# A decoder of two post-norm layers on one core: regrouped feed-forward weights, base products moved ahead, and transfers put behind the transposed input

## The reference

```python
x = _layernorm(x + _L0_attn_ref(...))   # down to 128, gelu, two passes of a bidirectional state-space mixer
                                        # with a 7-tap causal convolution, up to 512
x = _layernorm(x + _L0_xattn_ref(...))  # cross attention over the context joined with x: 16 heads of 96, 4 key heads
x = _layernorm(x + _L0_ffn_ref(...))    # gate, up (512 to 1792), silu, down; weights (int - zero) * scale
x = _layernorm(x + _L1_attn_ref(...))   # self attention, 32 heads of 16, alibi
x = _layernorm(x + _L1_xattn_ref(...))  # cross attention over the context: 32 heads of 128, 8 key heads, rms norms
x = _layernorm(x + _L1_ffn_ref(...))    # x @ W.T + b, plus a rank-16 adapter mixed over 8 experts by a router
```

## Time and profile before

| | us |
|---|---|
| median of 3 runs | 1679.01 |
| lowest and highest | 1676.1 and 1681.4 |
| the profiled execution, its own time | 1680.96 |
| its span, first to last instruction | 1679.2 |

### The profile page before, as it was taken

The page is one execution under the profiler, slowest core; times in us unless marked ns, Lnnn a source line. Parts: engine busy times, 40 slices in busy tenths (PEclk is TensorE's granted clock), DMA queues, the critical chain, the costliest instruction groups (busy, mean ns, idle before and its releaser), DMA issues. The chain is left out here.

```text
span 1679.2 us, 29888 instructions
## 1 busy us (share of the span) xinstructions
PE 1575.3 (94%) x11188; PEld 1316.2 (78%) x11188; DVE 932.6 (56%) x1647; ACT 803.6 (48%) x2447; POOL 769.3 (46%) x625
## 2 busy tenths in 40 slices
PE   6999999999997699998999879999999999999978
PEld 3777897888886488878777678888888888888866
DVE  3847503333365778775667734555555555555755
ACT  3342325444443355536999724454454454544520
POOL 3403214343421788842533545555555545554423
PEclk9999999999999799999999999999999999999999
DMA  6100200010102552203000031101101101100001
GB/s 207 38 1 1 57 20 20 20 41 2 52 2 82 182 175 98 79 1 120 1 2 26 29 113 38 39 26 38 46 19 51 38 27 39 32 26 14 1 1 51
DMA packets 62258, 77.85 MB, mean 46 GB/s; under 512 B 12136, under 2 KB 41316, under 8 KB 62116
## 3 DMA queue, kind: packets, MB, share of 16 engines
q1 hardware_dynamic: 61652, 74.63, 13.9%
q0 software_dynamic: 464, 1.32, 0.3%
HBM read 73.85 MB, written 2.10 MB: 45 GB/s over the span
## 5 line engine op out<-in xcount | busy, mean ns | idle before, releaser
L1145 POOL TENSOR_TENSOR xa_rs<-xa_ms,minus_half 128x5 f32<-128x5 f32 x64 | 74.7, 1168 | 170.0 <-DVE xa_ms L1395 169.9
L1151 POOL TENSOR_TENSOR xa_prob<-xa_prob,xa_inv 128x512 f32<-128x512 f32 x64 | 66.7, 1042 | 136.2 <-DVE xa_inv L1362 136.2
L763 POOL TENSOR_TENSOR xa_prob<-xa_prob,xa_inv 128x1024 f32<-128x1024 f32 x32 | 60.7, 1896 | 140.8 <-DVE xa_inv L1023 140.8
L1342 ACT ACTIVATE xa_prob<-xa_prob,xa_peak 128x128 f32<-128x128 f32 x256 | 99.7, 391 | 41.9 <-DVE xa_peak L1406 41.9
L1390 DVE TENSOR_REDUCE xa_ssq<-pre 128x4 f32<-128x512 f32 x64 | 43.9, 686 | 135.6 <-ACT pre L1328 135.6
L1699 DVE SCALAR_TENSOR_TENSOR ff_acc<-ff_ring,ff_sT,ff_acc 128x512 f32<-128x512 f32 x140 | 100.4, 747 | 21.6 <-ACT ff_acc L1653 12.7
L1599 PE MATMUL ff_ring<-xT_hi,ff_w 128*128 128x512 f32 x224 | 91.7, 410 | 18.1 <-DVE ff_acc L1699 13.5
L100 PE MATMUL xa_qp<-late_q_hi,xT_hi 128*128 128x512 f32 x256 | 107.2, 419 | 0.0
L1328 ACT ACTIVATE pre<-xa_qp 128x512 f32<-128x512 f32 x64 | 38.2, 597 | 142.6 <-PE xa_qp L102 142.6
L100 PE MATMUL xa_rows<-late_o_hi,xa_out_hi 128*128 128x512 f32 x256 | 102.6, 401 | 1.9 <-DVE xtok L1369 1.9
L2092 ACT ACTIVATE pre<-pre,sa_peak 128x128 f32<-128x128 f32 x256 | 99.2, 397 | 9.5 <-DVE sa_peak L2131 9.3
(11 more groups left out here) (415 smaller groups left out, 5054.6 us busy)
## 6 DMA issues: line engine op xcount, KB each, us to landing
pre<-in_wq SPq DMA_DIRECT2D x8, 1024.0 KB, 5.8
late_raw_o<-in_wo SPq DMA_DIRECT2D x8, 1024.0 KB, 5.2
ff_dn_q<-in_down_w SPq DMA_DIRECT2D x7, 512.0 KB, 3.8
ff_dn_z<-in_down_z SPq DMA_DIRECT2D x7, 512.0 KB, 4.9
ff_dn_s<-in_down_s SPq DMA_DIRECT2D x7, 512.0 KB, 6.1
pre<-in_wq SPq DMA_DIRECT2D x16, 192.0 KB, 3.5
pre<-in_wo SPq DMA_DIRECT2D x16, 192.0 KB, 3.9
pre<-in_xT SPq DMA_DIRECT2D x2, 1024.0 KB, 13.7
```

What stands on the lines that cost most here:

```text
L763: pool.tensor_tensor(prob[:, t % 3, :, :], prob[:, t % 3, :, :], bc(inv[:, t % 3, :], 2, [P, Q, KEYS]), ALU.mult).then_inc(s["norm"], 1)
L1145: pool.tensor_tensor(rs[:, :], ms[:, :], m.minus_half[:, 0:Q + 1], ALU.pow).then_inc(s["rs"], 1)
L1151: pool.tensor_tensor(prob[:, u % 2, :, :], prob[:, u % 2, :, :], bc(inv[:, u % 2, :], 2, [P, Q, S]), ALU.mult).then_inc(s["norm"], 1)
L1342: last = act.activation(prob[:, u % 2, h, :], prob[:, u % 2, h, :], ACT.Exp, bias=peak[:, u % 2, h:h + 1], accum_out=total[:, u % 2, h:h + 1])
```

## The change

It touches all six stages.

- Mixer: SP waits for the second half of `xT` (x1) before it issues `xtok`, `w_up` and `b_up`; POOL issues `taps` last, behind its small transfers and the constants, and after the same wait.
- First cross attention: the value weights are split in four pieces, the first products wait piece by piece, four fillers in place of nine.
- Feed-forward: the turns are grouped (0), (1, 2), (3, 4), (5), (6) in place of (0, 1), (2, 3), (4, 5), (6), so that there are 40 `out_rows` (16 of 12 matmuls, 24 of 6) in place of 32; SP issues the gate and up weights of turn T+1 ahead of the down weights of T; the weights' pieces are tied to units by two written tables; the first groups wait for turn 0's pieces one by one, two fillers in place of seven.
- Self attention: the output weights are split by DVE at the stage's head, no longer by ScalarE and POOL behind the first values.
- Second cross attention: the first key and value weights are split in two pieces; POOL's early pieces are spread over its steps 0 to 7; two fillers in place of five, and none in place of the 20; the base products of batches 0 to 3 of the last feed-forward replace the fillers at the end, one of them standing where there was no filler, in four banks that the two stages share.
- Last feed-forward: low rank first, then base(4), four `adapted`, and the rest in turn, five banks; the scaling of the norm is done by ScalarE, with a small shift from DVE (one column).

```diff
@@ hydra_stage, SP and POOL
                 sp_.dma_start(w_xbc[:, :], io["in_wT"][:, DIN:DIN + CONV]).then_inc(ld["in"], 16)
+                sp_.wait_ge(ld["x1"], 16)
                 sp_.dma_start(m.xtok[:, :, :], io["x"].rearrange("b s d -> s b d")).then_inc(ld["up"], 16)
...
-                pool.dma_start(taps[:, :, :], io["conv_w"].partition_broadcast(P)).then_inc(ld["conv"], 16)
                 pool.dma_start(conv_b[:, :], io["conv_b"].partition_broadcast(P)).then_inc(ld["small"], 16)
...
                 pool.memset(m.ones[:, :], 1.0).then_inc(s["consts"], 1)
 
+                pool.wait_ge(ld["x1"], 16)
+                pool.dma_start(taps[:, :, :], io["conv_w"].partition_broadcast(P)).then_inc(ld["conv"], 16)
                 pool.wait_ge(ld["conv"], 16)
@@ cross0_stage, TensorE (ScalarE and DVE split by c in the same way)
-                idle_products(pe, m, turn[:, 0:P], 9)
-                pe.wait_ge(s["v_lo"], 1)
+                idle_products(pe, m, turn[:, 0:P], 4)
                 for b in range(B):
-                    values_of(item(b)[:, 0:FEATS], m.cT_hi, m.cT_lo, b).then_inc(s["pre_mm"], 1)
+                    values_of(item(b)[:, 0:FEATS], m.cT_hi, m.cT_lo, b, b == 0).then_inc(s["pre_mm"], 1)
@@ ffn0_stage
-TABLE = [(hb, k) for hb in range(2 * math.ceil(TILES / GROUP)) for k in range(min(GROUP, TILES - GROUP * (hb // 2)))]
+GROUPS = ((0,), (1, 2), (3, 4), (5,), (6,))
+HALVES = 2 * len(GROUPS)
+TABLE = [(hb, k) for hb in range(HALVES) for k in range(MT * len(GROUPS[hb // 2]))]
...
-        mid = {n: [n - LAG] for n in range(LAG, 25)}
-        end = {}
-        mid[25], end[25], mid[26], end[26], mid[27], end[27] = [20, 21], [22], [23], [24], [25], [26, 27]
+        mid = {3: [0, 1], 4: [2, 3], 5: [4, 5], 6: [6, 7], **{n: [n - 1] for n in range(9, 22)}, 22: [22], 23: [24, 25], 24: [26, 27],
+               25: [28, 29], 26: [30, 31], 27: [32, 33]}
+        end = {21: [21], 22: [23], 27: [34, 35]}
...
+        weight_units = {1: (1, 1, 2, 2), 2: (3, 4, 4, 5), 3: (6, 7, 8, 9), 4: (10, 11, 12, 13), 5: (14, 15, 16, 17), 6: (18, 19, 20, 21)}
+        down_units = {0: (1, 1, 1, 2, 2, 2), 1: (3, 3, 4, 5, 5, 6), 2: (7, 7, 7, 8, 8, 8), 3: (10, 10, 11, 12, 12, 13),
+                      4: (14, 14, 15, 16, 16, 16), 5: (18, 18, 19, 20, 20, 21), 6: (22, 22, 23, 24, 24, 25)}
...
                 for T in range(TURNS):
+                    if T < TURNS - 1:
+                        if T >= 2:
+                            sp.wait_ge(s["w"], KC * (T - 1))
+                        elif T == 1:
+                            sp.wait_ge(s["w_first"], KC)
+                        ffn_stage_inputs(sp, io, *stage[(T + 1) % 2], T + 1, s["ld_even" if T % 2 else "ld_odd"])
                     if T:
-                        if T >= 3:
-                            sp.wait_ge(s["w"], KC * (T - 2))
-                        elif T == 2:
-                            sp.wait_ge(s["w_first"], KC)
-                        ffn_stage_inputs(sp, io, *stage[T % 2], T, s["ld_odd" if T % 2 else "ld_even"])
                         sp.wait_ge(s["dn_sub"], T)
                         sp.wait_ge(s["dn_w"], MT * T)
@@ cross1_stage, POOL's steps
-                        split_o(0, 2 * t)
-                        split_o(0, 2 * t + 1)
-                    if g <= G:
+                        split_o(0, t)
+                    if t == 2:
+                        split_o(0, 2)
+                        split_o(0, 3)
+                    if t == 3:
+                        split_kv(1, 0)
+                        split_kv(1, 1)
+                    if 4 <= t < B:
+                        split_q(1, b - 4)
+                        split_o(1, b - 4)
+                    if 1 < g <= G:
@@ cross1_stage, TensorE: unit 2, and behind the last unit
-                        idle_products(pe, m, rows[:, 0:P], 20)
+                        idle_products(pe, m, rows[:, 0:P], 0)
...
                 scores(UNITS - 1)
+                base(0, "qn", UNITS)
                 out_rows(UNITS - 3)
...
-                idle_products(pe, m, qp[:, 0:P], 9)
+                pe.wait_ge(s["kn"], UNITS)
+                base(1, "v_lo", UNITS)
                 out_rows(UNITS - 2)
...
-                idle_products(pe, m, qp[:, 0:P], 6)
+                base(2, "qT", UNITS)
                 out_rows(UNITS - 1)
                 turn_batch(UNITS - 2)
-                idle_products(pe, m, qp[:, 0:P], 14)
+                base(3, "masked", UNITS)
                 turn_batch(UNITS - 1)
@@ self_stage, DVE (taken from ScalarE and POOL)
+                dve.wait_ge(s["ld_o"], 16)
+                dve.tensor_copy(wo_hi[:, :, :], raw_o).then_inc(s["o_hi"], 1)
+                dve.wait_ge(s["o_hi"], 1)
+                dve.tensor_tensor(wo_lo[:, :, :], raw_o, raw(wo_hi[:, :, :]), ALU.subtract).then_inc(s["o_lo"], 1)
@@ lora_stage, TensorE and ScalarE
-                for b in range(1, B):
+                base(EARLY)
+                for b in range(EARLY):
+                    adapted(b)
+                for b in range(EARLY + 1, B):
+                    adapted(b - 1)
                     base(b)
-                    adapted(b - 1)
                 adapted(B - 1)
...
+                for b in range(B):
+                    act.wait_ge(s["shift"], b + 1)
+                    act.activation(m.xtok[:, b, :], m.xtok[:, b, :], ACT.Identity, bias=shift[:, b:b + 1],
+                                   scale=m.rstd[:, b:b + 1]).then_inc(n5["x"], 1)
```

More of the change, by code:

```diff
@@ L1061, in cross1_stage @@
         out_hi, out_lo = (sb(n, [P, 2, Q, S], F32R) for n in ("out_hi", "out_lo"))
-        qp, kvp, qt, kt, score, turn, mixed, rows = (pb(n) for n in ("qp", "kvp", "qt", "kt", "score", "turn", "mixed", "rows"))
+        qp, kvp, qt, score = m.late.bank
+        kt, turn, mixed, rows = (pb(n) for n in ("kt", "turn", "mixed", "rows"))
         s = {n: sem("xa1_" + n) for n in (
@@ L1643, in _ @@
                     turn(b)
-                    out_rows(28 + b)
+                    out_rows(LATE + b)
                 for b in range(4, B):
@@ L2179, in lora_stage @@
         low = [pb(f"low{i}") for i in range(2)]
-        rows = [pb(f"rows{i}") for i in range(BANKS)]
-        small, turned = pb("small"), pb("turned")
+        rows = [*m.late.bank, pb("rows4")]
+        small = pb("small")
+        turned = small[:, P:P + B]
+        shift = sb("shift", [P, B])
         s = {n: sem("lo_" + n) for n in (
-            "chain", "q", "logits", "lg", "exp", "wide", "wide_T", "route", "low", "t", "t_hi", "t_lo", "res", "rows", "add", "stored")}
+            "chain", "q", "logits", "lg", "exp", "wide", "wide_T", "route", "low", "t", "t_hi", "t_lo", "res", "rows", "add", "shift", "stored")}
         n5 = norm_sems(sem, "n5")
```

146 lines of the change are left out of this document (83 added, 63 removed).

## The result

The changed kernel takes 1653.26 us (median of 4 runs, 1649.81 to 1653.92), the kernel before 1677.78. The forecast was 1646.0, its range 1637 to 1656. The profiled execution of the changed kernel took 1649.81 us, its span is 1648.0.

A forecast was written before the change was run, and what follows sets the result against it. TensorE, busy 94% of the span, was taken as the bound, with gains only where it waits, runs fillers or runs slowly. Terms -2.7 - 2.3 - 9.8 + 0 - 9.2 - 9.0 = -33.0 gave median 1646.0 us, range 1637 to 1656.

The forecast's parts named there:

- Mixer's head: Mixer start: without taps in front the transposed input lands 2.9 us earlier, the residual about on the edge; -2.7 us.
- First cross attention: Its head: with value weights in quarters TensorE starts at about 172.1 in place of 174.33; -2.3 us.
- the signs: What the changed profile would show, such as first product at 11.5 to 12 and first values 2.3 us into their stage.
- Feed-forward: Its head, the largest term: earlier weights shorten the waits, fillers at 730.8 in place of 740.6; -9.8 us.
- the next hold: Feed-forward units 7 to 9: POOL's five instructions each in 7 and 8 delay row 8; 6.3 us lost.
- Self attention: Two instructions, some 3.6 us, move to DVE, which waits there; POOL loses one nothing waited for; 0 us.
- Second cross attention's head: Earlier start 1.0, unit 2's wait for POOL 6.9, clock behind it 1.5, less 0.2; -9.2 us.
- Joint and end: Last two stages: base products replace fillers; second cross attention ends 3.3 us later, the kernel's end 9.0 us earlier.
- signs that were to show it wrong: A residual landing after 28, a wait in units 10 to 27, or bases running at 0.43 us a matmul.
- more comes back: Rival: POOL's hold in feed-forward units 7 to 9 is hidden, -6 us, giving 1639 to 1641; chance 0.12.
- the hold only moves: Rival: feed-forward down weights land at 550, turns up to 3 wait, gain 3 for 9.8: 1653; chance 0.12.
- clock: Rival: with fewer fillers TensorE stands idle and its clock falls, 7 us at four places: 1653; chance 0.10.

The follow-up runs named there:

- taps_first: The changed kernel with the taps issued as POOL's first transfer again, SP's wait kept: 1653.64 us (one run).
- again: The changed kernel measured once more without an edit: 1651.84 us (5 runs), ratio 0.9838 to the kernel before.
- res_early: The changed kernel with SP's wait taken out, so the residual input is not held back; taps stay behind their wait: 1650.68 us, ratio 0.9833.
- mixer_hold: Changed kernel with residual step at second pass's head, POOL's context low parts behind first-pass roots, down-weight steps of turns 1 and 2 spread: 1645.92 us.

## Why the prediction came out as it did

The forecast of -33.0 stands against -27.0 over many profiles and -26.7 in the medians. By its own steps:

- **Mixer's head, -2.7: measured -1.0, and that is luck.** The start was right: 10.5 to 11.9 us in place of 14.56 and 13.67, in the mean 11.2 for 14.1, the 2.9 of the text, and `taps_first` shows that the taps are the cause. The context's transfer moved with it (issued at 20.99 for 23.80). What failed is "the residual is then complete at 24.5 to 25": it came at 27.5 to 28.65 where DVE waited for it, near the bound of 28.8 that the text gave. And the step did not ask what POOL's 4.44 us do to DVE when they move from 18 to 24 us. The text gave `w_conv` "until the convolution" and looked at TensorE alone. `again` and `res_early` show the hold, 4.20 and 3.67 us. So the second pass begins at 94.8 in the mean, before and after: the head gave nothing. The 1.0 lies behind it, where the first profile of before takes 75.9 us, with a clock of 0.50 from 125 to 130, and the other eight 73.8 to 74.1.
- **First cross attention, -2.3: measured -2.0**, by the mechanism named: 360.88 to 360.93 in eleven profiles, 362.43 in one, whose head ran at the lower clock (363.06 and 363.09 before). The first values stand 1.15 us into the stage, as 172.1 in the sum has it; the 2.3 among the signs is the gain and not this time.
- **Feed-forward, -9.8: measured -7.3, 6.8 when undone.** The start, DVE's wait at the down weights (forecast 2.6, measured 1.3) and TensorE's behind it (4.6; 3.20 to 4.83 in eight profiles) came where the text had them, DVE's half as long, and so did the next hold: row 3 ends 34.7 us into the stage, 34.0 by the text. The hold is a little larger: from row 7's end (576.65) to row 8's (597.99) are 21.3 us for 60 matmuls (14.0), 7.3 lost where the term had 6.3, and 0.5 more between rows 3 and 7. That profile's stage is 8.2 shorter than before. The mean is 1.2 longer than it, by the clock behind row 8's wait, low in five of eight profiles; the term had none.
- **Self attention, 0: measured +0.2.** The +1.4 of the two profiles is the clock, since both kernels show both lengths, the long one with 0.83 where the short one has 1.00.
- **Second cross attention's head, -9.2: measured -8.1** (656.76 - 651.97 + 3.3). The two key/value halves brought the first product forward by 0.97. The release by POOL gave 7.0, 6.9 expected (11.6 to 4.6 us from the root). The 1.5 us for the clock were right in size (627.02 against 625.45 behind the release in the two profiles of before) but read from one execution: of three profiles with the fillers and the old steps two have the low clock (0.57 and 0.58) and one has 1.00, so that part is worth about 1.0 on average. The rest that is missing lies ahead of POOL's root: the first transposed probabilities stand 22.3 to 22.5 us into the stage in four profiles and 23.6 to 23.8 in seven, and in `again` some of the first products (seven from 4.5 us into the stage on) take 0.43 us each where they take 0.23 in the first profile.
- **Joint and end, -9.0: measured -8.7.** The second cross attention's end was +3.3 in the profiles, as forecast. From first product to last sum are 25.1 to 25.2 us, the forecast's 25.1, in five of ten profiles, and 26.25 in the other five. The difference is how long the first products of low rank run at 0.43 us each: 4.8 us in the first profile, 3.1 in `again`.

The 6.0 us too much are thus the mixer (1.7), the feed-forward (2.5), the head of the second cross attention (1.1) and small parts. Of the signs that were to show it wrong, three came in part: the residual landed after 28 in four of the six profiles in which DVE waits for it, TensorE waits 0.66 us for POOL's low part in unit 17 (648.24), and the low-rank products, though not the bases, ran at 0.43 us. The rest of the distance from 1646.0 to 1653.26 is that the median of four runs lies 1.2 us above that of all nine. Of the rivals, *more comes back* is refuted; *the hold only moves* and *clock* each describe a part of what is missing, neither alone the 7 us that it claimed. Fewer fillers did not make the clock worse: the mean granted clock is 0.981 and 0.982 in the two profiles of before and 0.984 and 0.986 in those of after.

What stays open: why the chip grants 2.4 GHz behind a wait in one execution and 1.2 in the next. Only that it does was shown. Why the last stage is long where the second cross attention is short stays open too. That the fillers of unit 2 are useless by themselves was not tried alone, nor were the edits of the first cross attention and of self attention; what is said of these two rests on their stage lengths.

## What to carry to other kernels

Where a transfer is put back, follow every instruction that it releases, on all engines: POOL's product moved by 6 us into DVE's stretch, the residual landed later, and together they took back all that TensorE's earlier start gave. Look in the trace of before for instructions far longer than others of their shape: DVE's 2.21 us over 8 columns, 0.17 in `mixer_hold`, was a price that could be read, and taking such pairs apart, with SP's wait out, was worth another 5 us. Don't price the granted clock from a single profile; take two, and count only what both show.

## What was unexpected of the hardware

- DVE and POOL can hold each other until the other's instruction ends, both ways: 4.20 us for 0.17 on DVE, 4.69 for 0.55 on POOL. The profile shows the held instruction as busy, not as waiting.
- The clock behind the same wait differs between executions of the same program: 1.00 or 0.50 over 5 us, worth up to 2.8 us from there to the feed-forward's end (153.5 and 156.3). Stages fall into separate lengths, 214.5 to 214.7 and 215.8 to 216.6 us for self attention.
